# First layer of a two-layer transformer: order of the early loads, network products, and query transfers

## The reference, cut to what matters

```python
xn = layernorm(x)
q, k, v = split(xn @ Wqkv.T + b)          # 16 query heads of 16, ONE key and value head
a = softmax(causal(q @ k.T / 4)) @ v @ out_w.T + out_b
f = (silu(xn @ Wg.T) * (xn @ Wu.T)) @ Wd.T       # Wg, Wu: 704 x 256, int weights - 128, times a scale
x = x + a + f
# second layer: 16 heads of 128 with block-scaled weights, and a routed network of 16 experts beside a shared one
```

## Time and profile before

| | us |
|---|---|
| median of 3 runs | 1143.99 (1140.02 to 1145.54) |
| the profiled execution | 1144.49, of which the span is 1142.8 |
| first step of the first layer begins | 34.87 |
| PE busy | 1061.8 (93%) |
| DVE, ACT, POOL busy | 826.1, 688.7, 511.2 |

### The profile page before, as it was taken

The page is one execution under the profiler, slowest core; times in us unless marked ns, Lnnn a source line. Parts: engine busy times, 40 slices in busy tenths (PEclk is TensorE's granted clock), DMA queues, the critical chain, the costliest instruction groups (busy, mean ns, idle before and its releaser), DMA issues.

```text
span 1142.8 us, 21332 instructions
## 1 busy us (share of the span) xinstructions
PE 1061.8 (93%) x7410; PEld 971.6 (85%) x7410; DVE 826.1 (72%) x1600; ACT 688.7 (60%) x1921; POOL 511.2 (45%) x578
## 2 busy tenths in 40 slices
PE   8778799899699789999999999999999999999996
PEld 7568679779678679888999989999999899899996
DVE  6677687777577566888777767677777676777775
ACT  3676566766476444555666666676666665555553
POOL 4586655654565100005854434444343443588200
PEclk9799999999899999999999999999999999999999
DMA  7656746746653465643544454443445443333120
GB/s 243 171 148 189 185 158 191 199 149 193 165 188 101 133 202 161 196 163 120 186 124 145 127 172 145 140 139 124 154 136 169 127 150 93 106 102 110 59 93 19
DMA packets 138167, 167.87 MB, mean 147 GB/s; under 512 B 10917, under 2 KB 103205, under 8 KB 137037
## 3 DMA queue, kind: packets, MB, share of 16 engines
q1 hardware_dynamic: 134989, 158.11, 45.7%
q0 software_dynamic: 3072, 8.39, 2.2%
HBM read 118.10 MB, written 48.37 MB: 146 GB/s over the span
## 4 chain that ended last, share of the span: by engine, by line
PE 60%; POOL 12%; DVE 8%; DMA 6%; issue 6%; ACT 4%; SPq 3%; DVEq 0%; POOLq 0%; ACTq 0%
PE ps_m L1672 24%; PE ps_s L1672 10%; PE ps_t L1672 6%; DMA d_w_head<-parts 4%; PE ps_b L1672 3%; POOL d_xs L1321 3%; PE ps_b L847 3%; PE ps_c L1672 2%; PE ps_t L1788 2%; PE ps_c L1788 2%; POOL parts L443 2%; POOL codes L445 2%; POOL parts L447 2%; ACT probs L498 1%; PE ps_m L847 1%
## 5 line engine op out<-in xcount | busy, mean ns | idle before, releaser
L1672 PE MATMUL ps_m<-xTa,w_qk 128*128 128x512 f32 x768 | 200.3, 400 | 6.8 <-DMA xTa<-d_xn1T 3.9
L1433 ACT ACTIVATE probs_a<-ps_s,neg_max_a 128x256 f32<-128x256 f32 x256 | 118.0, 473 | 144.9 <-DVE neg_max_a L1638 144.9
L1672 PEld LDWEIGHTS ps_m<-xTa,w_qk 128*128 128x128 f32 x768 | 137.6, 189 | 37.3 <-DVE v L1491 4.6
L498 ACT ACTIVATE probs<-ps_s,neg_max 128x128 f32<-128x128 f32 (+1 forms) x256 | 104.9, 420 | 58.5 <-DVE neg_max L789 57.1
L1334 POOL CAST we_down<-raw_down_e 88x512 fp32r<-88x512 f32 x47 | 28.6, 608 | 219.4 <-DMA raw_down_e<-in_we_down 219.4
L1638 DVE TENSOR_REDUCE neg_max_a<-ps_s 128x2 f32<-128x512 f32 x128 | 88.1, 690 | 51.5 <-PE ps_s L1672 49.8
L1672 PE MATMUL ps_m<-w_v,xTa 128*128 128x256 f32 x768 | 106.1, 288 | 0.0
L1672 PE MATMUL ps_t<-pTa,v 128*128 128x256 f32 x768 | 103.5, 284 | 0.0
L1672 PE MATMUL ps_s<-kTa,qTa 128*128 128x256 f32 x768 | 102.9, 283 | 0.3 <-DVE kTa L1469 0.2
L1672 PEld LDWEIGHTS ps_s<-kTa,qTa 128*128 128x128 f32 x768 | 96.7, 191 | 1.0 <-DVE kTa L1469 0.7
L1672 PEld LDWEIGHTS ps_t<-pTa,v 128*128 128x128 f32 x768 | 96.9, 191 | 0.1
(11 more groups left out here) (245 smaller groups left out, 2800.0 us busy)
## 6 DMA issues: line engine op xcount, KB each, us to landing
w_qk<-d_w_head SPq DMA_DIRECT2D x64, 512.0 KB, 3.8
raw_up<-in_we_up SPq DMA_DIRECT2D x47, 352.0 KB, 3.4
d_w_head<-parts SPq DMA_DIRECT2D x128, 128.0 KB, 2.4
raw_down_e<-in_we_down SPq DMA_DIRECT2D x47, 176.0 KB
codes<-in_w_codes SPq DMA_DIRECT2D x64, 128.0 KB
scales<-in_w_scales SPq DMA_DIRECT2D x64, 128.0 KB
q<-d_q_scr SPq DMA_DIRECT2D x32, 256.0 KB, 5.6
d_xs<-zeros SPq DMA_DIRECT2D x16, 384.0 KB, 6.2
```

The source lines that it names most:

```text
L498: last = act.activation(probs[:, g % 3, a * w:(a + 1) * w], ps_s[g % 2][:, a * w:(a + 1) * w], ACT.Exp, bias=neg_max[:, g % 2, a:a + 1], s ...
L1433: last = act.activation(probs[:, s, t, :], ps_s[s][:, t * SEQ:(t + 1) * SEQ], ACT.Exp, bias=neg_max[:, s, t:t + 1], scale=1.0, accum_out=s ...
L1672: last = pe.matmul(out, lhs[i], rhs[j], start=start and n == 0, stop=stop and n == 2, skip_group_check=True)
```

## The change

Seven edits, all in the first layer.

1. `EARLY` is 6: six network items stay ahead of the first step, and six stand in the first turn, at steps 1, 3, 5, 7, 9, 11 (before: two, at 3 and 5), the flush at 12 (before 7).
2. SP issues the first turn's query stores and loads after two chunks of loads; chunks 2 and 3 and the late weights follow.
3. `raw_down` lies where a later tile of the second norm lies, and no longer where the split probabilities do; ACT's wait for it in the first step is gone. The conversion of `w_down` and the waits for the late weights move from steps 0 and 1 to step 5.
4. In later turns a chunk's work on SP comes ahead of the query transfers of its step: the second store goes behind the chunk of step 18, the first sequence's load to step 20, the second's to step 2 of the next turn (behind that step's chunk).
5. `BIAS_AT`: the bias is added at steps 11, 11, 9 of turns 1, 2, 3 (before 5, 5, 3).
6. `LAST_FREE`: in the last turn the steps without a split are 5, 15, 16 (before 3, 9, 14, 15, 16), so the last split is at step 18, not 20.
7. `warm(16)` and `warm(4)` in place of `warm(24)` and `warm(8)`.

```diff
-    nc.sbuf_base = region_probs
+    nc.sbuf_base = region_sums
     raw_down = sb("raw_down", [P, len(HT), D], I32)
...
-    EARLY = 10
+    EARLY = 6
...
-    FFN_AT = [(3, 5, 7)] + [(1, 2, 5, 6, 7, 8, 10, 11, 12, 13, 14, 15, 16)] * (TURNS - 1)
+    FFN_AT = [(1, 3, 5, 7, 9, 11, 12)] + [(1, 2, 5, 6, 7, 8, 10, 11, 12, 13, 14, 15, 16)] * (TURNS - 1)
...
-    LAST_FREE = (3, 9, 14, 15, 16)
-    BIAS_AT = (0, 5, 5, 3)
+    LAST_FREE = (5, 15, 16)
+    BIAS_AT = (0, 11, 11, 9)
...
-    OUT_WEIGHTS, LATE_AT, LATE_LOADS = 1, 1, 6
+    OUT_WEIGHTS, LATE_AT, LATE_LOADS = 1, 5, 6
...
-        for n in range(AHEAD):
+        for n in range(2):
             load_chunk(n)
-        late_loads = [(raw_down, "w_down"), (raw_o, "w_o"), (raw_s2, "w_s2"), (raw_gw, "w_gw"), (raw_s13, "w_s13")]
-        for dst, name in late_loads:
-            sp.dma_start(dst[:], dram[name]).then_inc(late_in, 16)
...
         load_q(0, 0)
         load_q(0, 1)
+        for n in range(2, AHEAD):
+            load_chunk(n)
+        late_loads = [(raw_down, "w_down"), (raw_o, "w_o"), (raw_s2, "w_s2"), (raw_gw, "w_gw"), (raw_s13, "w_s13")]
+        for dst, name in late_loads:
+            sp.dma_start(dst[:], dram[name]).then_inc(late_in, 16)
...
-            if n == 0 and p:
-                load_q(p, 1)
-            if n in (17, 18) and p + 1 < TURNS:
-                store_q(p + 1, n - 17)
-            if n == 18 and p + 1 < TURNS:
-                load_q(p + 1, 0)
+            if n == 17 and p + 1 < TURNS:
+                store_q(p + 1, 0)
             if chunk_of(p, n) is not None:
                 chunk(p * CHUNKS + chunk_of(p, n))
+            if n == 18 and p + 1 < TURNS:
+                store_q(p + 1, 1)
+            if n == 20 and p + 1 < TURNS:
+                load_q(p + 1, 0)
+            if n == 2 and p:
+                load_q(p, 1)
...
-            if g == 0:
-                act.wait_ge(down_ready, 1)
...
-            if g == 0:
+            if g == LATE_AT:
                 dve.wait_ge(late_in, 16 * LATE_LOADS)
...
-        warm(24)
+        warm(16)
...
-                warm(8)
+                warm(4)
```

More of the change, by code:

```diff
@@ L373, in sync @@
         sp.dma_start(ob[:], dram["out_b"].partition_broadcast(P)).then_inc(ob_in, 16)
-        for n in range(AHEAD):
+        for n in range(2):
             load_chunk(n)
-        late_loads = [(raw_down, "w_down"), (raw_o, "w_o"), (raw_s2, "w_s2"), (raw_gw, "w_gw"), (raw_s13, "w_s13")]
-        for dst, name in late_loads:
-            sp.dma_start(dst[:], dram[name]).then_inc(late_in, 16)
-        sp.dma_start(s_down[:], dram["s_down"].rearrange("(a n) -> a n", a=1).partition_broadcast(P)).then_inc(late_in, 16)
         for i in range(2):
@@ L385, in sync @@
         load_q(0, 1)
+        for n in range(2, AHEAD):
[3 more added lines that the diff above has]
+            sp.dma_start(dst[:], dram[name]).then_inc(late_in, 16)
+        sp.dma_start(s_down[:], dram["s_down"].rearrange("(a n) -> a n", a=1).partition_broadcast(P)).then_inc(late_in, 16)
         load_x(1)
```

## The result

| | before | after |
|---|---|---|
| median of 20 runs, us | 1142.98 | 1145.41 |
| lowest to highest | 1140.02 to 1145.54 | 1141.11 to 1149.93 |
| profiled execution; its span | 1144.49; 1142.8 | 1143.02; 1141.3 |
| first scores of the first step | 34.87 | 27.63 |

The ratio after to before is 1.0021, with a 95% interval of 1.0011 to 1.003: about 2.4 us slower, where 11.5 us faster was forecast (1132.5 against the 1143.99 of the first three runs), and outside the range of 1125 to 1141. The interval leaves equality out, though the difference is under the 0.5% that was called measurable.

The account below looks back on a forecast made before the run. Second layer bound by PE, first-layer changes passing whole to the end. First turn -7.5 + 3.8 + 0.6, bounces + 4.3 + 0.5, POOL waits - 4.2 - 0.7 - 8.5: -11.7 us, 1132.5; middle 8 in 10 1125 to 1141.

Parts of the forecast that it names:

- The first step: Start of turn 0: queries bounced sooner, so first scores at 27.3 instead of 34.87, 7.5 us earlier; bounds 5 and 9.
- The waits on POOL: PE's waits in turns 1, 2, 3 end as stores no longer queue behind query loads: -4.2, -0.7, -8.5 us.
- The early fall of the clock: Rival, start of first turn: less warming halves PE's clock at 11 us, bounce 3.7 us later, 1136.5; chance 0.11.
- the late weights at step 5: First turn: loads landed by the wait at about 43 us, so nothing counted; 2 us if they land late.
- The term of the bounce: First scores of turn 1: PE waits 4.3 us for queries loaded behind step 19's chunk; bounds 2.5 and 6.
- one such stretch goes in turn 1 and one comes, so this is even: Turn 1: half-clock stretches after PE waits of about 4 us, one removed and one added, counted as no net change.
- The bounces into turns 2 and 3: Query loads for the first scores of turns 2 and 3: 0.5 us lost for both, bounds 0 and 3.
- the late load hits every bounce: Rival: POOL delays step 19's split, so all three query loads cost 7 us each, 1149; chance 0.07.
- The term of POOL: First turn, output product of step 14: POOL's low part comes late, costing 0.6 us; 3 if chunk 0's store lands at 46.
- the waits on POOL only move: Rival, later turns: step 2's query load delays the next chunks' stores, half of 13.4 us returns, 1139.5; chance 0.17.
- the prediction's own sign of being wrong: First turn, steps 5 to 14: the forecast fails if PE waits there for `hT` or the late weights.
- The products: First turn: four network items moved inside cost 2.0 us for one, 0.6 for each other; 3.8 in all, bounds 1 and 6.

Follow-up runs that it names:

- the last kernel: Against the 0.9858 version (query load ahead, ten early items, chunk 0's store first): second query store ahead of step 18's chunk, load right behind that chunk; 0.9868 of before.

## Why the prediction was wrong

**Right, by its own steps.** The first step: first scores forecast at 27.3, measured at 27.63, and the loads issued at 20.65 for 20.1. By step 14, ahead of the output product, the turn was to be ahead by 3.7 (7.5 less 3.8), and was by 2.8. The waits on POOL: -4.2, -0.7 and -8.5 forecast, -5.3, -1.9 and -8.4 measured, with the 7.76 us gone; the cause given, stores queued behind a load of queries, is borne out by the kernel with edit 4 alone. The early fall of the clock didn't come (granted clock 1.00 in every window from 5 to 28 us), and the late weights at step 5 cost nothing.

**The term of the bounce was mis-sized, and this turned the sign.** "From the first issue of such a group it takes 1.3 us to the last issue and up to 6.0 to its landing": that is a row of a load that had no chunk right ahead of it on the queue, though zeros and chunks stood behind it. The edit itself puts a chunk's stores and loads right ahead, and a load in such a place, up to 8.6 us, was there to be read in the same trace. From the first issue to the scores it took 9.8 us, and 10.3 with edit 4 alone. That makes the wait 6.42 where 4.3 was forecast, and 7.43 with edit 4 alone. The second half of the error is the clock: "one such stretch goes in turn 1 and one comes, so this is even". Behind 6.42 us PE ran at 0.50 (window of 114 to 118), and by (1,1) the bounce had cost 9.3. That the clock makes up the whole difference between a wait and its shift is my reading; no run separates it. I had charged the half clock in one place where three bounces each bring a wait of over 3 us: 9.3, 5.2 and 3.7 make 18.2, against 4.8.

The bounces into turns 2 and 3 were to land "at 285.9 against scores at 285.41", half a microsecond late. The same wrong 7.3 us stands in that sum: with 9.8 it gives 3 us late, and 3.52 and 3.16 were measured. The rival that "the late load hits every bounce" was closest to what came at the bounces, with 7 us each and 1149, at a chance of 0.07; its cause, POOL late for the split of step 19, was not the one, since the kernel with edit 4 alone has no such delay and the dearest wait.

The Trainium skill ("DMA: Bandwidth & Descriptors", section "Rules for kernel authors") says to issue a DMA early, do the compute and wait late. By it edit 4 would only lose. Measured by itself it lost on balance, 1.005, but it also gave the 5.0 and 8.3 us at POOL's waits that the rule leaves out. By the order on the queue these come from the second sequence's load, which stays behind the stores of a turn's first two chunks in every kernel here with edit 4; what had to be issued earlier was the first sequence's load, and with that ahead of the chunk of step 19 the gains stay and most of the loss goes.

**The term of POOL was mis-sized.** "So POOL costs 0.6 us more", with the store landing "at 43 to 44", bounds 0 and 3. Split 2 began at 46.69, beyond the bound at 46, and the term came out at 5.3: at (0,14) the shift is -2.8, at (0,15) +2.5, the wait of 3.37 and the half clock behind it. POOL's own work was right: from the start of split 2 to the end of the sixth block 27.5 us were forecast, and 27.8 came. The bytes were about right too (257 GB/s in 21 to 46.7). Left out was SP itself, which was held up for 4.37 us at the issue of the zeros and then got the second store of chunk 0 out at 39.6; and the half clock behind the wait. The kernel with the late loads behind puts the late weights' share at about 3 us of the 5. The kernel with chunk 0's early store shows that the wait moves to the next store if only one is freed. It is the rival "the waits on POOL only move", on another store than the one it named, and the prediction's own sign of being wrong, a wait of PE for `hT` at steps 5 to 14 of the first turn.

**The products.** 3.8 us given back was forecast, and 4.9 came up to step 14 (from -7.7 to -2.8), inside the bounds of 1 and 6. But their blocks on POOL are what PE waits for at the output product. With the late weights ahead of a store the edit loses, some 4 us; with the late weights behind, six, eight and ten items are not told apart.

**Left out.** "Edits 5 and 6 beyond that: nothing counted": 0.9967 by itself for the splits, since the wait of 3.9 us for `xTa` goes. And "I let what the first layer gains or loses pass to the end whole" was wrong by 5.6 us: of +8.3 at the end of the first layer +2.7 arrived. Some 4 of that is edit 6, the rest a fall of the clock at 426 us that before has and after has not. Of the other kernels some have it and some don't, and what decides it is open.

The small total is thus no sign of small terms: -5.6 us that the prediction didn't count hide part of a first layer that ended 8.3 us late.

## What to carry to other kernels

In these traces a transfer's time went with its place on the queue. When a load is moved, price its landing with what will stand around it then, and not with the row of its old place; here some 2.5 us more from issue to scores, three times, with the clock behind it, was the main part of what turned a forecast of 1% faster into no gain. Look in the trace at hand for a transfer that already stands in such a place. Charge a wait of PE with more than its length: the four of 3.2 to 6.4 us here moved the steps by 1.2 to 1.6 times that. And when work is moved out of a wait into the stretch behind it, ask which engine is next in line there (POOL here): freeing it of one store only moved its wait to the next. And compare edits by repeated times: two single traces here differ by 4 us at one step for kernels whose times can't be told apart.

## What the runs showed of the hardware

- Of four loads of 256 KB the slowest took 6.0 us from issue to landing with no chunk right ahead on the queue, and 4.8 and 5.4 in such places in two kernels after. Right behind a chunk's stores and loads it took 8.6 in the kernel before, 8.3 in after, 8.9 with edit 4 alone, and 8.9 in the last kernel. Other transfers stood behind the loads in all of these.
- The issue of a transfer can hold up its engine: that of the zeros (384 KB) took 4.37 us on SP's queue, behind some 5 MB of loads, where other single issues are 0.49 and 0.56 and one of two stores 0.88 (at 112 to 114 us in the kernel before).
- Waits of PE of 3.37 and 6.42 us were each followed by a stretch at a granted clock of 0.50 (windows of 76 to 80 and 114 to 118), and 1.00 was back in 80 to 84. A third to a half less warming at the start changed nothing in the times that could be measured (0.9893 and 0.9891).
